# Expert weights cast to bf16 in DRAM during attention and loaded through ACT's queue

## The reference

```
q, k, v = xn @ Wq, xn @ Wk, xn @ Wv            # 4 heads of 256, 256, 512
g = log_sigmoid(xn @ Wgk1 @ Wgk2 + b) / 16
S_t = exp(g_t) * S_{t-1} + k_t^T v_t ;  o_t = q_t @ S_t / 16
o = rmsnorm(o) * silu(xn @ Wg) ;  attention = o @ Wo

top 2 of 4 experts by xn @ gate_W, weights by softmax
expert_e(xn) = ln(relu(ln(xn @ W1[e] + b1) * g1 + be1) @ W2[e] + b2) * g2 + be2
experts = xn + sum of the two, weighted
```

## Time and profile before

| | |
|---|---|
| median of 3 runs | 1209.06 us (1207.42 to 1212.25) |
| the profiled execution, its own time | 1210.35 us |
| its span on the slowest core (core 0) | 1208.2 us |
| spans of the even cores | 1208.2, 1207.8, 1205.1, 1207.3 us |
| spans of the odd cores | 1181.5, 1188.6, 1193.4, 1191.2 us |
| TensorE busy on core 0 | 1005.1 us, 83% |
| VectorE, ScalarE, POOL busy | 613.4, 538.9, 226.0 us |
| queue q0 (POOL) | 84.55 MB, 37.7% of the DMA engines' span |

### The profile page before, as it was taken

One profiled execution on the slowest core, in us unless ns is written; L12 is line 12 of the kernel. 1 busy time (PEld: TensorE's weight loads), 2 busy tenths in 40 slices (PEclk: granted clock), 3 DMA queues, 4 the chain that ended last, 5 costly groups with the idle time before them and its releaser, 6 DMA issues.

```text
span 1208.2 us, 21526 instructions; the slowest of 8 cores (1181.5 to 1208.2 us)
## 1 busy us (share of the span) xinstructions
PE 1005.1 (83%) x4822; PEld 437.6 (36%) x4822; DVE 613.4 (51%) x1259; ACT 538.9 (45%) x1128; POOL 226.0 (19%) x271
## 2 busy tenths in 40 slices
PE   1588896889788988899688989897589999969983
PEld 1243333434333433344233334342234444424431
DVE  2224763643476347643676411125266766646772
ACT  3335443543554435343332211206276676747772
POOL 6000000000000000001033370104134332312321
PEclk9799997899999989999989999998799999989996
DMA  9996132430333152228237999869799977755744
GB/s 212 165 199 116 45 79 62 95 80 15 100 79 84 31 119 50 61 53 140 53 79 191 264 319 237 228 169 148 131 142 186 157 121 127 130 104 97 127 76 70
DMA packets 164301, 149.26 MB, mean 124 GB/s; under 512 B 119580, under 2 KB 131916, under 8 KB 164144
## 3 DMA queue, kind: packets, MB, share of 16 engines
q0 software_dynamic: 40624, 84.55, 37.7%
q1 hardware_dynamic: 120960, 53.76, 21.4%
q10 hardware_dynamic: 2592, 9.44, 2.5%
HBM read 111.58 MB, written 44.93 MB: 130 GB/s over the span
## 4 chain that ended last, share of the span: by engine, by line
PE 54%; DMA 14%; ACT 9%; issue 9%; DVE 9%; POOL 1%; SPq 1%; DVEq 1%; ACTq 0%; POOLq 0%
PE pb L453 36%; PE pb L1647 16%; DMA s_xr<-x_tm 5%; DMA s_xgT<-s_xg 3%; DMA s_wg<-Wg 3%; ACT s_hT L1731 2%; DMA s_kdT<-s_kd 1%; DMA out<-s_xr 1%; DVE s_L L982 1%; ACT s_z L1755 1%; PE pb L458 1%; DVE s_W L1107 1%; SPq L467 1%; PE pb L1669 1%; ACT s_sq L1113 1%
## 5 line engine op out<-in xcount | busy, mean ns | idle before, releaser
L1647 PE MATMUL pb<-s_we,s_xgT 128*128 x624 | 149.1, 394 | 39.8 <-DMA s_xgT<-s_xg 21.1
L453 PE MATMUL pb<-s_wv,s_xnT 128*128 128x512 bf16 x576 | 146.3, 402 | 23.6 <-ACT s_v L1057 12.1
L1647 PE MATMUL pb<-s_we,s_hT 128*128 x624 | 148.7, 381 | 0.0
L453 PE MATMUL pb<-s_wo,s_ogl 128*128 128x512 bf16 x576 | 133.5, 386 | 12.4 <-DMA s_ogl<-og_d 3.9
L453 PE MATMUL pb<-s_wg,s_xnT 128*128 128x512 bf16 x576 | 129.5, 383 | 10.6 <-DMA s_wg<-Wg 10.3
L1107 DVE SCALAR_TENSOR_TENSOR s_W<-s_W,s_eb,pb 128x512 bf16<-128x512 bf16 x144 | 100.9, 742 | 45.1 <-PE pb L453 44.6
L1731 ACT ACTIVATE s_hT<-pb,s_gbs 128x128 bf16<-128x128 bf16 x312 | 116.7, 459 | 4.6 <-PE pb L458 4.6
L1767 POOL DMA_INDIRECT out<-s_y,s_list x39 | 61.7, 1583 | 256.3 <-DVE s_rf L1692 170.8
L1647 PEld LDWEIGHTS pb<-s_we,s_xgT 128*128 128x128 bf16 x624 | 62.1, 101 | 118.6 <-issue 60.2
L1755 ACT ACTIVATE s_z<-pb,s_rf 128x512 bf16<-128x512 f32 x78 | 56.5, 774 | 102.0 <-DVE s_rf L1692 102.0
L453 PEld LDWEIGHTS pb<-s_wv,s_xnT 128*128 128x128 bf16 x576 | 55.7, 102 | 105.0 <-issue 53.2
(11 more groups left out here) (182 smaller groups left out, 1283.1 us busy)
## 6 DMA issues: line engine op xcount, KB each, us to landing
s_we<-W POOLq DMA_DIRECT2D x64, 256.0 KB, 15.6
s_xr<-x_tm ACTq DMA_DIRECT2D x18, 512.0 KB, 7.9
out<-s_xr SPq DMA_DIRECT2D x18, 512.0 KB, 7.8
s_ogl<-og_d SPq DMA_DIRECT2D x16, 512.0 KB, 10.4
s_x<-x_tm POOLq DMA_DIRECT2D x12, 512.0 KB, 5.7
og_d<-s_ogT POOLq DMA_DIRECT2D x12, 512.0 KB, 3.0
s_wg<-Wg POOLq DMA_DIRECT2D x4, 1024.0 KB, 38.8
s_wv<-Wv POOLq DMA_DIRECT2D x4, 1024.0 KB, 66.4
```

What stands on the lines that cost most here:

```text
L453: lambda e: e.matmul(out=out, lhsT=lhsT, rhs=rhs, start=start, stop=stop),
L1647: t = P.emit("tensor", lambda e, dc=dc: e.matmul(out=ps, lhsT=lhs[:, dc, :], rhs=P.window("tensor", e, ("w", s, hf), s_we[layer][dc], 512) ...
```

## The change

- A new DRAM tensor `wb_d` holds all expert weights in bf16.
- `cast_e(i)` has POOL issue one DMA from DRAM to DRAM, of 256 rows of W1 or W2 (1 MB in float32, 0.5 MB in bf16), on a semaphore of the expert, `d_wb[e]`. There are 32 of them, eight per expert. They are issued ahead of the units: none in block 0, one per unit in blocks 1 and 4, three per unit in blocks 2 and 3.
- `load_e` is issued by ACT in place of POOL, from `wb_d`, without a cast. The first piece of each call waits for the eight casts of its expert.
- Experts 0, 1 and 2 are loaded in `wo_run`, behind the load of the next tile's x: expert 0 in tiles 3 to 6 and expert 1 in tiles 7 to 10 with four pieces each, expert 2 in tiles 11 to 13 with 6, 5 and 5. Expert 3 is issued at the end of steps 0 to 3, four pieces each.
- The gathers of slots 4, 5 and 6 are issued ahead of `step(0)`, behind `load_b2`.

```diff
+    wb_d = dt("wb_d", [2 * NE * D, D], BF16).ap()
...
+    d_wb = [mksem(f"d_wb{e}") for e in range(NE)]
+    cast = []
+    def cast_e(i):
+        n = D // 4
+        e, l, q = i // 8, i // 4 % 2, i % 4
+        cast.append(i)
+        gdma(wb_d[i * n:(i + 1) * n, :], (W1, W2)[l][e, q * n:(q + 1) * n, :], d_wb[e])
+
     def load_e(e, wait, part=range(16)):
-        o = e_off[e] // 2
         for i in part:
             l, dc = i // NDC, i % NDC
-            gdma(s_we[l][dc].ap[:, o:o + D],
-                 (W1, W2)[l][e, dc * 128:(dc + 1) * 128, :], d_e[e],
-                 wait=wait if i == 0 else [])
+            row = (2 * e + l) * D + dc * 128
+            P.emit("scalar", lambda x, l=l, dc=dc, row=row: x.dma_start(
+                out=s_we[l][dc].ap[:, e_off[e] // 2:e_off[e] // 2 + D],
+                in_=wb_d[row:row + 128, :]),
+                wait=(list(wait) + [(d_wb[e], 8 * 16)]) if i == part[0] else [], inc=d_e[e],
+                inck=16)
...
+            for _ in range(0 if b == 0 else 1 if b in (1, NB - 1) else 3):
+                cast_e(len(cast))
             unit(u, side)
...
-    load_e(0, [proj_te[NB - 1]])
...
-                load_e(1, [])
...
             if q + 1 < NT:
                 wo_load(q + 1)
+            if q < 7:
+                load_e(0, [proj_te[NB - 1]], range(4 * q - 12, 4 * q - 8))
+            elif q < 11:
+                load_e(1, att_done, range(4 * q - 28, 4 * q - 24))
+            elif q < 14:
+                load_e(2, att_done, range((16 * (q - 11) + 2) // 3, (16 * (q - 10) + 2) // 3))
...
     load_b2(att_done)
+    for s in range(4, 7):
+        f_gather(s)
     load_vec(2, s_g2, g2b, wo_done)
     def step(s, n):
-        if s < 4:
-            load_e(2, [], range(4 * s, 4 * s + 4))
         own, th = s < n, 1 <= s <= n
-        if 4 <= s + 3 < n:
+        if 7 <= s + 3 < n:
             f_gather(s + 3)
...
-        if s >= 4:
-            load_e(3, [], range(2 * s - 8, min(2 * s - 6, 16)))
+        if s < 4:
+            load_e(3, wo_done, range(4 * s, 4 * s + 4))
```

## The result

| | before | after |
|---|---|---|
| median | 1210.21 us of 4 runs | 1198.03 us of 4 runs (1196.3 to 1201.28) |
| ratio | | 0.9899, 95% interval 0.9869 to 0.9928 |
| profiled execution | 1210.35 us | 1196.3 us |

The change makes the kernel 1.0% faster, 12 us where 28 were forecast. In a later measurement with five rounds on another chip the ratio was 0.9862 (0.9846 to 0.9878). Some executions are longer because the cores of one die show a lower granted clock; all ratios leave these out, and of the second profile of the change, which is one of them, only cores 4 and 6 are read.

The account below looks back on a forecast made before the run. Bound by TensorE plus stalls from full DMA between 700 and 910 us. Gross gain 36.9 less costs 6.0 gives -30.9 on core 0: 1179.4, plus 3 for another core, less 1.3 to the median: 1181 us, range 1168 to 1198.

Parts of the forecast that it names:

- Removed slot stalls: Experts' slots: TensorE's waits for transposes of gathered rows go, 25.2 us gained; costs of 1 and 1 us set against it.
- Prices of the DMA work: All DMA engines: a 0.52 MB cast takes 2.9 us, bf16 pieces 2.8 to 3.2 us per MB.
- The residue of Wo: Wo: of 11.7 us lost to late s_ogl and x, 2.5 us stay lost; bounds 0 and 11.7.
- the sum: Wo, per tile: x, store and s_ogl loads 4.7 us plus four pieces 3.2 us, 7.9 of 7.9 us, just full.
- The sign that I had named: Wo, tiles 4 to 13: distance between two activations of s_xr under 7.9 us if the change works.
- s_ogl was to go: Wo: the wait for attention's output loads and the slow matmuls behind it disappear, 5.4 us gained.
- x was to be on time: Wo: the late x and the matmuls slowed behind it disappear, 6.3 us gained.
- Rival 1: Wo: DMA engines still full, everything lost there stays lost, s_ogl and x late as before; 1190 us, chance 0.17.
- The last block: Last attention block: unit 0's cast queues behind the load of Wo, where no cover is left; 1.5 us lost.
- Start and end: Stretches before the last attention block and in the last slots: the prediction has no term for them.
- Rival 2: Attention: casts take double, each of eight groups of three costs 2 us, +16 us in all; 1197 us, chance 0.08.
- The added 3 us for another core: Kernel's end: another even core, such as core 6 with less to give back, may finish last; 1179.4 becomes 1182.4 us.

Follow-up runs that it names:

- Gathers alone: Kernel before with only the gathers of slots 4 to 6 issued ahead of step 0, no casts, weights loaded as before: ratio 0.9894 to the kernel before.
- an early load: Changed kernel with block 3's load of s_ogl issued ahead of attention's last transposes: ratio 0.9831 to the kernel before.
- casts alone: Kernel before with the 32 casts added and nothing that reads them: ratio 1.0072 to the kernel before.
- core 6 above: Changed kernel with 64-row casts kept off Wo's load on own and neighbour cores, x two tiles ahead, s_ogl early: Wo 147.5 us on core 6, ratio 0.9826.
- x two ahead: Changed kernel with the x of a tile in Wo issued two tiles ahead instead of one: ratio 0.986 to the kernel before.
- four casts: Changed kernel with only block 1's four casts, all experts loaded from those 1024 rows (wrong weights): ratio 0.9831 to the kernel before.

## Why the prediction was wrong

**Removed slot stalls (25.2 us, less 2 for costs): right.** Forecast -23.2, measured -23.5; for core 6, with 5.1 us less to give back, 18.1, and it gave 18.1. Gathers alone gave 17.7 of it on core 0, so the place of the gathers was the main cause, as argued from the earlier trace rows.

**Prices of the DMA work: right.** A cast was priced at 2.9 us of all engines. 12 of them raised the share of 123 us from 0.28 to 0.59, which is 38 us or 3.2 us each; q0 alone went from 11.2% to 39.0%, 2.8 us each. The rest is in q1, whose 14784 packets, as many as before, took 19.5% instead of 16.6%. Casts in blocks 2 and 3 cost nothing. Pieces in bf16 were priced at 2.8 to 3.2 us per MB and took 3.1.

**The residue of Wo (2.5 us of 11.7): this is the step that failed.** I forecast -9.2 us for the stage and got +4.2, 13.4 of the 17.1 us that core 0 missed its forecast by. The DMA work of the stage fell by the 8 to 9 us forecast; what failed is the step from the sum to the wait, that work which fits in the tile leaves only 2.5 us of lateness. The sum said nothing of order. The sign that I had named, under 7.9 us between two scalings of x in tiles 4 to 13, failed too: those of tiles 6, 7 and 8 are 12.2 and 15.7 us apart. By parts:
- s_ogl was to go (-5.4). The slow issue on SP, which I read from the earlier trace rows, did go. But the new kernel starts its pieces in tile 3 and issues more of them while these four loads are under way; before, the last piece of expert 0 landed at 695.9 us, 1.4 us after the last of these loads was issued, and the next piece was issued at 716.7. It cost +3.8 instead. Pieces from tile 5 on took the wait away, an early load too. The casts have a share in it, as casts alone show.
- x was to be on time (-6.3): the late ones of tiles 11 to 13 went, -6.5, as forecast. New ones came in tiles 8 and 9, +4.0: the x of tile 8 was issued at 727.10 us and landed after 15.5 us. It landed about as late on the other even cores, behind pieces in its own queue and beside other transfers; no run tells these apart.
- In tile 0 the same wait of 3.40 us is followed by 6.35 us of matmuls instead of 3.61, +2.8 us at the lower clock: the granted clock of these matmuls is 0.56, mostly the level of 1.2 GHz, where it was 1.00. All four even cores have 11.0 to 11.2 us for this tile against 8.4 before. It comes and goes in the other kernels, once even in the gathers alone (11.1 on core 6), so what sets it is open.

Rival 1, everything in Wo stays lost, came nearest in kind and was still too mild: it lets the stage gain 0. The rule of the Trainium skill beneath it (DMA: Bandwidth & Descriptors, Issuing engines are not separate DMA queues: another issuing engine saves only issue time) was the better guide than my sum. But it was not fullness alone that cost: core 6 above loses nothing at 0.92.

**The last block (1.5 us, bounds 0 to 2.9): under-sized.** It took 3.2 on core 0, 3.3 to 3.5 on the others. The mechanism was named rightly, s_kdT behind Wo: it landed after 19.2 us instead of 17.6, and its wait rose from 0.2 to 1.9 us with slower matmuls behind. It is not the whole: core 0 took 136.2 us once without that wait, and what set that is open. What I missed is whose casts stretch the load of Wo. I counted the one of the own core. The runs show the odd cores', three per unit in the same microseconds.

**Start and end (0): +1.4 and +0.9.** Not looked into. The casts are not needed for the late start: in gathers alone, which has none, the last block starts at 518.8 to 521.1 us, in the changed kernel at 518.0 to 520.8, before at 516.6 to 518.3. Rival 2, attention pays, did not happen in blocks 2 and 3, where I had put it, but it is real where cover is short: block 1 with two casts per unit lost 10 to 14 us on three cores. With one per unit it is still a risk. Block 1 took 94.1 to 94.4 us in the changed kernel's first profile, but 103.9 on one core with x two ahead, 99.6 on one with four casts, and 100.1 on core 4 in the second profile of the change; the kernels without casts have 94.1 to 94.5. That may be why its runs vary; it is not shown.

**The added 3 us for another core** were not wanted for the reason given: core 0 was the slowest again, with 4 and 6 within 0.5 us.

## What to carry to other kernels

A stage sum of DMA work tells whether transfers fit, not whether the urgent ones land in time: list for each new burst which loads with a reader waiting are under way in the same microseconds, and start it after them. Price an edit in several parts by its cheapest part first; here three lines with the gathers gave most of what the whole change did. Large DRAM to DRAM transfers belong where neither the core itself nor its neighbours have a load or transpose without cover. And when a row of a profile merges several issues, look at the time of one before calling the engine held.

## What the runs showed of the hardware

- Casts on the odd cores lengthened a load of the even cores (four pieces of Wo) from 24.2 to 24.6 us to 27.7 to 31.9, without any cast of the even cores; with theirs it took 28.9 to 31.6, and 23.9 to 24.6 with none on either side.
- A cast from DRAM to DRAM of 1 MB in float32 took 2.8 us of all engines in its own queue, 3.2 with what it added to others. Packets of the queue with casts and x loads took 0.57 us on average, those of the queue with the transposes 0.05. Two transposes issued beside two casts held SP for 17.20 us.
- A wait of the same 3.40 us was followed by 16 matmuls that took 3.61 us in one kernel (granted clock 1.00) and 6.35 in another (0.56).
- VectorE stood 14 us with both of its inputs ready, at a DMA share near full, in the kernel before as in changed ones; the profile names no cause.
- 32 casts that nothing reads cost 9 us, none of it in the two blocks in which the core issues 24 of them.
